# Bf16 parts that add up in PSUM, and a first spread whose chain of steps reaches over three groups, in a four-layer graph network on one core

## The reference

```
# 1: three message layers (l = 0, 1, 2)
m = relu(concat([x[src], x[dst], ew]) @ edge_W[l] + edge_b[l])
agg = segment_sum(m, dst)
x = relu(concat([x, agg]) @ node_W[l] + node_b[l])
# 2: eight relations
h0 = relu(x @ W_enc + b_enc)
agg = segment_sum(einsum('nd,rdo->rno', h0, W_rel)[etypes, src], dst)
out = h0 + relu(agg + h0 @ W_self + bias)
# 3: twice, a mean over the neighbours
agg = segment_sum(h[src], dst) * inv_deg[:, None]
h = relu(agg @ Wl + b + h @ Wr)
# 4: two layers of attention with two heads
h = layernorm(ent)
scores = leaky_relu(s_h[src] + s_t[dst] + s_r[edge_type])
A = 0.85 * segment_softmax(scores, src)
Z = h for both heads
for _ in range(3):
    Z = segment_sum(A[:, :, None] * Z[dst], src) + 0.15 * h
ent = Z.reshape(n, 128) @ W_o[l] + x
```

## Time and profile before

| What | Value |
|---|---|
| Time, median of 3 runs | 15644.12 us (15627.54 to 15644.18) |
| The profiled execution's own time | 15644.36 us |
| Its span, first to last instruction | 15642.6 us |
| PE busy | 13044.7 us, 83% |
| PEld busy | 11579.5 us, 74% |
| DVE busy | 11612.7 us, 74% |
| ACT busy | 4436.1 us, 28% |
| POOL busy | 2355.9 us, 15% |
| Mean granted TensorE clock | 0.907 |

### The profile page before, as it was taken

How to read it: one execution, slowest core, us unless ns; L and a number is a source line. 1 busy time by engine, 2 the same in 40 slices (tenths; PEclk the granted TensorE clock), 3 DMA queues, 4 the chain that set the end, 5 groups by cost and what they waited for, 6 DMA issues and landing times. The chain is left out here.

```text
span 15642.6 us, 488871 instructions
## 1 busy us (share of the span) xinstructions
PE 13044.7 (83%) x112911; PEld 11579.5 (74%) x112912; DVE 11612.7 (74%) x41655; ACT 4436.1 (28%) x16100; POOL 2355.9 (15%) x7659
## 2 busy tenths in 40 slices
PE   3444698998986999999867889899997788889998
PEld 2444587887875999989833778789993377778998
DVE  5444697997984888767679555589998955558999
ACT  1000122221221222222223232345542322224554
POOL 2777000000000000000000010112220000001221
PEclk9999998998996999999989786799998977779999
DMA  1111342442430111222235222222224522222222
GB/s 50 46 47 40 92 115 77 114 114 77 114 90 13 39 39 36 68 59 70 56 105 145 71 63 58 63 65 73 71 64 115 142 60 61 59 59 65 73 71 63
DMA packets 1260835, 1134.60 MB, mean 73 GB/s; under 512 B 224351, under 2 KB 1240800, under 8 KB 1260106
## 3 DMA queue, kind: packets, MB, share of 16 engines
q1 hardware_dynamic: 1234954, 1130.19, 27.5%
q0 software_dynamic: 25792, 3.35, 0.2%
HBM read 1115.06 MB, written 17.86 MB: 72 GB/s over the span
## 5 line engine op out<-in xcount | busy, mean ns | idle before, releaser
L965 DVE TENSOR_SCALAR hotT<-idx,iota_col 128x512 bf16<-128x512 f16 (+1 forms) x6000 | 1870.5, 365 | 605.9 <-PE G L1173 372.5
L1578 PE MATMUL G<-u_b,hotT 128*128 x6000 | 1682.2, 388 | 487.1 <-DVE msgs L1489 436.7
L972 DVE TENSOR_SCALAR hot<-iota_row,place 128x128 f32<-128x128 f16 (+1 forms) x9000 | 1909.8, 276 | 23.7 <-PE acc L1181 1.7
L1721 ACT ACTIVATE msgs<-G,share 128x64 f32<-128x64 f32 x6000 | 1394.6, 315 | 1346.6 <-PE G L1735 1346.1
L1578 PEld LDWEIGHTS G<-u_b,hotT 128*128 128x128 f32 x6000 | 1136.7, 237 | 671.0 <-issue 666.6
L1735 PE MATMUL G<-u_b,hotT 128*128 x12000 | 1591.1, 276 | 50.0 <-DVE hotT L1669 50.0
L1057 PE MATMUL G<-table_m,hotT 128*128 x9000 | 1424.2, 248 | 194.2 <-DVE sums L1079 166.5
L1745 PE MATMUL S<-msgs,hot 128*128 128x128 f32 x12000 | 1586.0, 275 | 0.0
L1735 PEld LDWEIGHTS G<-u_b,hotT 128*128 128x128 f32 x12000 | 1466.3, 193 | 50.7 <-issue 50.7
L1745 PEld LDWEIGHTS S<-msgs,hot 128*128 128x128 f32 x12000 | 1461.9, 192 | 0.0
L1069 PE MATMUL acc<-msgs,hot 128*128 128x102 f32 x9000 | 1386.5, 277 | 0.5 <-ACT msgs L1087 0.5
(11 more groups left out here) (321 smaller groups left out, 22667.8 us busy)
## 6 DMA issues: line engine op xcount, KB each, us to landing
idx<-pos_rows SPq DMA_DIRECT2D x7875, 128.0 KB
key_b<-key_rows SPq DMA_DIRECT2D x62, 416.0 KB
ty_b<-type_rows SPq DMA_DIRECT2D x62, 416.0 KB
rows<-rel_rows SPq DMA_DIRECT2D x1500, 6.0 KB
ew_now<-ew_rows_d SPq DMA_DIRECT2D x1125, 3.0 KB
sorted_d<-recs,place POOLq DMA_INDIRECT x806
sorted_d<-empty SPq DMA_DIRECT2D x4, 1500.0 KB
e<-sorted_d SPq DMA_DIRECT2D x1, 6000.0 KB
```

The lines of the kernel that those rows point to most:

```text
L965: op = eng.tensor_scalar(hotT[:, c % 2, n], idx[:, c, r], p.col[:, first:first + 1], None, ALU.is_equal)
L972: op = eng.tensor_scalar(hot[:, c % 2, q], p.row16[:], place[:, c % 2, q:q + 1], None, ALU.is_equal)
L1578: eng.matmul(G[c % 2][:, at_k:at_k + W], hotT[:, c % 2, q * P:(q + 1) * P], table[:, ds(dst_at(at, q, 24 * W), W)], start=True, stop=False)
L1721: op = eng.activation(msgs[:, c % 2, 2 + j // HEADS, j % HEADS * D:(j % HEADS + 1) * D], G[c % 2][1][:, j * D:(j + 1) * D], ACT.Copy, scal ...
```

## The change

1. **Message passes.** A gather is no longer three matmuls of 192 columns for a chunk but seven of 64: for each side the three parts are multiplied one after the other and add up in the same 64 columns of `G`. The edge weight keeps one matmul, of 64 columns: `ew_now` carries nine rows (three parts of the weight by three parts of its coefficient, `we9`), so the step's DMA brings nine rows. DVE's tensor reduce goes, and with it `sums` and the semaphore `taken`; ACT applies the relu to all four chunks in one instruction. A step is no longer cut in halves (H = 1).
2. **`relation_pass` becomes `parts_pass`**, with messages of 64 columns, not 102, and ACT writes them in one contiguous run for each chunk. The neighbour passes use it too: `sage_net` splits the table into three bf16 parts ahead of each pass, gathers in bf16 with 192 columns and scatters the three parts (12 bf16 matmuls in a step in place of four fp32 ones).
3. **First spread.** Four `G` tiles of one bank take turns in place of two of two banks; the gather of step t waits for the products of step t - 4. ACT does all products (eight instructions in a step), for step t - 2, and the exponential of step t - 1; DVE bends and subtracts for step t - 1; the scatter belongs to step t - 3. The own terms and the relation's are matmuls of 64 columns; the columns that are not needed are zero or not read.
4. **Later spreads.** The table is split into three bf16 parts ahead of each pass (`table_u`), `hotT` is bf16, and a gather is three bf16 matmuls of 128 columns for a chunk in place of one fp32 matmul.

```
-EW = 3
+EW = 9
...
             for q in range(4):
+                G = env["G"][c % 2][:, q * D:(q + 1) * D]
                 for side in range(2):
+                    of = dst_at(at, q, LAST) * 2 if side else src_at(at, 24 * 3 * D)
+                    for i in range(3):
+                        eng.matmul(G, env["hotT"][:, c % 2, side, q * P:(q + 1) * P], s.table3[side][:, ds(of + i * D, D)],
+                                   start=(side + i == 0), stop=False)
+                mm = eng.matmul(G, s.ew_now[:, c, q * P:(q + 1) * P], s.we9[:, l, :], start=False, stop=True)
...
         def scalar(eng, t, c, env):
+            env["later"](eng, env["gathered"], env["g0"], t + 1)
+            env["later"](eng, env["scattered"], env["sc0"], t - 3)
+            eng.activation(msgs[:, c, :, 0:D], env["G"][c % 2][:, 0:4 * D].rearrange("p (k f) -> p k f", f=D), ACT.Relu
+                           ).then_inc(env["made"].h, 1)
...
+def parts_pass(p, s, row, tables):
+        msgs = p.sb("msgs", [P, 4, 2, 3, D], BF16, ctx)
...
         for i in range(2):
-            neighbour_pass(p, s, s.cat[:].rearrange("p b f -> p (b f)"))
+            on_vector(p, [lambda e: e.tensor_copy(u[:], a)])
+            split_stage(p, u[:], [wide[:].rearrange("p (b q f) -> p b q f", q=3, f=D)[:, :, q, :] for q in range(3)])
+            parts_pass(p, s, s.pos_rows[0], [wide])
...
-        G = [p.ps("G", [P, 1024], ctx) for _ in range(2)]
+        G = [p.ps("G", [P, 512], ctx) for _ in range(4)]
...
                 def step(t, c):
+                    if not isinstance(t, int) or t > 1:
+                        product(t - 2, (c - 2) % 4)
                     if not isinstance(t, int) or t > 0:
-                        product(t - 1, (c - 1) % 4)
+                        share(t - 1, (c - 1) % 4)
                     pick(t, c)
-                    share(t, c)
...
+                    reach(eng, made, m0, t - 3)
+                    for q in range(4):
+                        to = G[c][:, q * W:(q + 1) * W]
+                        eng.matmul(to, hotT[:, c % 2, q * P:(q + 1) * P],
+                                   table[:, ds(dst_at(at, q, 24 * W), W)], start=True, stop=False)
+                        for i in range(3):
+                            eng.matmul(to[:, D:2 * D], near[:, c % 2, q * P:(q + 1) * P],
+                                       s.own[:, ds(src_at(at, 24 * SMALL) + i * 2 * HEADS, D)], start=False, stop=False)
+                        mm = eng.matmul(to[:, D:2 * D], rows[:, c, q], s.picks[:], start=False, stop=True)
...
-        hotT = p.sb("hotT", [P, 2, 4 * P], FP32, ctx)
+        hotT = p.sb("hotT", [P, 2, 4 * P], BF16, ctx)
+        table = p.sb("table_u", [P, BLK * 3 * W], BF16, ctx)
+        split_stage(p, out, [table[:].rearrange("p (b q f) -> p b q f", q=3, f=W)[:, :, q, :] for q in range(3)])
...
-                            mm = eng.matmul(G[c % 2][b][:, k * W:(k + 1) * W], hotT[:, c % 2, q * P:(q + 1) * P],
-                                            table[:, ds(dst_at(at, q, 24 * W), W)], start=True, stop=True)
+                            for i in range(3):
+                                mm = eng.matmul(G[c % 2][b][:, k * W:(k + 1) * W], hotT[:, c % 2, q * P:(q + 1) * P],
+                                                table[:, ds(dst_at(at, q, 24 * W) * 3 + i * W, W)], start=(i == 0), stop=(i == 2))
```

More of the change, by code:

```diff
@@ L1063, in gather @@
             return mm
         def scatter(eng, c, h, at, env):
-            j = (2 * (c - 1) + h) % 4
-            for k in range(2):
-                q = 2 * h + k
-                mm = eng.matmul(env["acc"][:, ds(dst_at(at, q, LAST), WIDE)], env["hot"][:, (c - 1) % 2, q, :], msgs[:, j, k, :],
-                                start=False, stop=False, skip_group_check=True)
-            return mm
-        def vector(eng, t, c, env):
-            for h in range(2):
-                j = (2 * c + h) % 4
-                env["later"](eng, env["made"], env["m0"], t * 2 + h - 3)
-                env["later"](eng, env["gathered"], env["g0"], t * 2 + h + 1)
-                eng.tensor_reduce(sums[:, j], env["G"][h][:, 0:6 * D].rearrange("p (k q f) -> p k f q", q=3, f=D),
-                                  AX.X, ALU.add).then_inc(env["taken"].h, 1)
@@ L1082, in scalar @@
-        def scalar(eng, t, c, env):
-            for h in range(2):
-                j = (2 * c + h) % 4
-                env["later"](eng, env["taken"], env["t0"], t * 2 + h + 1)
-                env["later"](eng, env["scattered"], env["sc0"], t * 2 + h - 3)
-                eng.activation(msgs[:, j, :, 0:D], sums[:, j], ACT.Relu).then_inc(env["made"].h, 1)
+            for q in range(4):
+                mm = eng.matmul(env["acc"][:, ds(dst_at(at, q, LAST), WIDE)], env["hot"][:, (c - 1) % 2, q, :],
+                                msgs[:, (c - 1) % 4, q, :], start=False, stop=False, skip_group_check=True)
@@ L1123, in scatter @@
                 for part in range(3):
-                    mm = eng.matmul(env["acc"][:, ds(dst_at(at, q, LAST), WIDE)], env["hot"][:, (c - 1) % 2, q, :],
-                                    msgs[:, j, k, part], start=False, stop=False,
-                                    skip_group_check=True)
+                    mm = eng.matmul(env["acc"][:, ds(dst_at(at, q, LAST), D)], env["hot"][:, (c - 1) % 2, q, :],
+                                    msgs[:, j, k, part], start=False, stop=False, skip_group_check=True)
             return mm
@@ L1133, in scalar @@
                 env["later"](eng, env["scattered"], env["sc0"], t * 2 + h - 3)
-                op = eng.copy(msgs[:, j, :, :, 0:D], env["G"][h][:, 0:6 * D].rearrange("p (k q f) -> p k q f", q=3, f=D))
+                op = eng.copy(msgs[:, j].rearrange("p k q f -> p k (q f)"),
+                              env["G"][h][:, 0:6 * D].rearrange("p (k f) -> p k f", f=3 * D))
                 op.then_inc(env["made"].h, 1)
-        edge_pass(p, s, [s.pos_rows[2]], None, 1, BF16, 0, FIVE, [(0, r) for r in range(RELS)], gather, scatter,
+        edge_pass(p, s, [row], None, 1, BF16, 0, FIVE, [(0, r) for r in range(NT)], gather, scatter,
                   lambda c: [p.ps("G", [P, 512], c) for _ in range(2)], None, scalar, {"scalar": sums_out(p, s)},
@@ L1419, in first_spread @@
             turned, hots, placed, shared, scattered, folded, termed, bends, lessed, kept))
-        g0, m0 = [x.at for x in gathered], [x.at for x in made]
+        g0, m0 = gathered.at, made.at
         on_vector(p, [lambda e: e.memset(rows[:], 0.0)])
@@ L1509, in _ @@
                 quarters(eng, step)
+                scatter_hots(Q - 2, (Q - 2) % 4)
+                bend(Q - 1, (Q - 1) % 4)
+                lessen(Q - 1, (Q - 1) % 4)
                 scatter_hots(Q - 1, (Q - 1) % 4)
-                product(Q - 1, (Q - 1) % 4)
-                for t in range(Q - 3, Q):
-                    fold(t, t % 4)
+                for t in range(Q - 4, Q):
+                    fold(t, t % 4, block_of(t))
                 turned.at += Q
@@ L1518, in _ @@
                 folded.at += Q + 1
-                made[0].at += Q
                 eng.wait_ge(folded.h, folded.at)
@@ L1566, in _ @@
                 shared.at += Q
-                made[1].at += Q
+                made.at += Q
             @block.tensor
@@ L1599, in step @@
                     gather(t, c, load_words(p, eng, 2, t, 1))
-                    if not isinstance(t, int) or t >= 2:
-                        scatter(t - 2, (c - 2) % 4)
+                    if not isinstance(t, int) or t >= 3:
+                        scatter(t - 3, (c - 3) % 4)
                 quarters(eng, step)
-                for t in range(Q - 2, Q):
+                for t in range(Q - 3, Q):
                     scatter(t, t % 4)
                 scattered.at += Q
-                for b in range(2):
-                    gathered[b].at += Q
+                gathered.at += Q
 def spread_pass(p, s, out):
     ctx = ExitStack()
-    table = out.rearrange("p b f -> p (b f)")
     W = HEADS * D
```

156 lines of the change are left out of this document (52 added, 104 removed).

## The result

The changed kernel takes **16,743.5 us** (median of 3 runs, 16,737.5 to 16,750.4) against 15,644.1: the ratio is 1.0707, interval 1.0682 to 1.0731. That is 1099 us slower; 1069 were forecast, and the time lies in the range. The profiled execution has a span of 16,748.7 us beside the 15,642.6 of before.

What follows compares the result with a forecast made beforehand. It took PE's sequencer (0.118 us an address) to bound the changed message passes and later spreads, and a ring of waits the old first spreads: 1200 + 1264 - 60 - 100 - 1245 + 10 = +1069, so 16,710 us, range 16,250 to 17,400.

Steps and rivals of the forecast that it cites:

- The price of an address: PE's sequencer: 0.118 us for each address instruction, read from four matmuls in the maximum pass.
- Message passes: Three passes: ten more address instructions a step, 3.40 us a step, +1200 us (bounds +1100 and +1340).
- Later spreads: Four passes: 12 addresses a step in place of 4, 2.60 us a step plus splits, +1264 us.
- Relation pass: Scatters of 64 columns, not 102, with PE being the bound: -60 us (0 to -75).
- Neighbour passes: Two passes: sequencer sets the step, 1.75 us against 1.91, less copy and splits: -100 us (+20 to -300).
- First spreads: Two passes: ring cut, PE sets the step at 2.75 us, full clock: -1245 us (-1340 to -910).
- the 5% added for waits that still meet: First spreads: allowance on PE's 2.62 us a step, giving 2.75.
- the ring: First spread: gather, pick, bend, exponential, product, gather of the step after next; cutting it lets PE set the step.
- The clock: Rival: thinly filled PE gets 1.2 GHz; +860 us in all spreads at all times, 17,570 us; chance in the spreads 0.07.
- The rival of hidden addresses: Whole kernel: sequencer runs ahead, engines decide; 13,130 us; chance 0.08 in full, 0.06 in part.
- The start: Ahead of the first message pass: nine rows of weights in place of three, twelve DMAs more, +10 us.
- The sum: Whole kernel: all parts together +1069 us on 15644.4, so 16,710 us, 6.8% more.

Runs made afterwards that it cites:

- narrow_own: Kernel of both_undone with the first spreads' score matmuls at their old widths (4 and 2 columns, not 64): 14,367.3 us, ratio 0.9046.
- ring_again: Changed kernel, but in the first spreads PE's gather of step t waits for products of step t - 2, not t - 4: 18,121.5 us.
- ring_narrow: Kernel of ring_again with the score matmuls also at their old widths, 4 and 2 columns: 18,082.4 us.
- msg_sums: Changed kernel with only the three message passes written as before (192-column gathers, reduce on DVE, three rows of weights): 15,503.3 us.
- both_undone: Changed kernel with its message passes and four later spreads written as before: 14,157.6 us, ratio 0.9058 to the kernel before.

## Why the prediction was right, step by step

**The price of an address** was right, and the sum rests on it. 0.118 us was read from four matmuls in another pass; the two runs with fewer addresses bear it out, with 0.122 between starts in the later spreads and 0.127 for each in the message passes. That the sequencer had nearly nothing to spare in the message passes was right too: ten addresses raised the step by 1.08 us where their price by the forecast is 1.18; that the rest is PE's wait for the sums, 0.16 a step, which is gone, was not tested by itself.

**Message passes**, +1200 forecast and +1227 measured: right. One reading in it was wrong. DVE's rest was worked out as its busy time less the reduce, 847.8 - 389.9. The groups of DVE overlap, however: 389.9 + 325.8 + 227.2 is 943 us beside a busy time of 848. What is left without the reduce is the other two groups, 559 us, as it came. It cost nothing, since DVE is far from the bound. ACT's work in the first spread was worked out in the same way, 2.24 us a step, and came as 2.01.

**Later spreads**, +1264 and +1331: the mechanism was right and the term too small. A step takes 2.64 us and not 2.60; the split has its place in the 14 us more ahead of the first matmul, as forecast. The term stood between its bounds.

**Relation pass**, -60 and -35. The price of a 64-column matmul was right: six of them take 0.34 us, (0.34 - 0.193) / 5 = 0.029. What was wrong was to take PE as the only bound. Timeline of PE in the relation pass after:

```profile
6224.91 1.48 PE L1101 MATMUL G<-wide,hotT 128*128 x16
6226.23 0.34 PE L1111 MATMUL acc<-msgs,hot 128*128 128x64 bf16 x6
6226.78 1.69 PE L1101 MATMUL G<-wide,hotT 128*128 x16 [0.21 <-issue]
...
6228.48 1.48 PE L1101 MATMUL G<-wide,hotT 128*128 x16
...
6229.97 1.48 PE L1101 MATMUL G<-wide,hotT 128*128 x16
```

Halves start 1.49 us apart where nothing comes between (6228.48 to 6229.97), and 1.87 where PE waits for issue (6224.91 to 6226.78), so part of the 0.2 us that PE was spared in a step went to its sequencer. Half was gained.

**Neighbour passes**, -100 and -64: a step takes 1.78 us, not 1.75, and the stretch of 715 us that the sum set it against holds 6 us around the pass. The two splits with the copy take 17 us as against 19. That it isn't PE's work is shown by the four steps above; which wait beside the addresses makes the 0.03 was not tested.

**First spreads**, -1245 and -1380: the mechanism was right, the size wrong mostly by the 5% added for waits that still meet. There are none: 2.62 us was PE's sum, 2.595 was measured. Here, where each handover has a whole step and PE never runs dry, the waits needed no allowance. The forecast gave the ring's cutting all the gain and full clock; the runs show that cutting it alone is enough for both, since narrow_own keeps 0.99, although 209 of the 1380 us hang on the clock alone in the ring.

**The clock** fell in the message and neighbour passes, to 0.89 and 0.78, as its rival had it, and cost little, as the prediction worked out: PE has time to spare there. In the spreads it stayed at 0.99 to 1.00. The prediction took it that idle time and the lower level go together in the ring; ring_again, idle for 423 of 1535 us at 0.99, shows that idle time alone doesn't bring it. The rival's price for all spreads at all times, +860, was too low as summed: it holds the four later spreads and the message passes, and leaves out the first spreads, whose 2.62 us a step would double too. The rival of hidden addresses was a little too high: 3 x 375 x 1.74 is 670 less for the message passes, not 640. The Trainium skill, same page, section "Part 1: The HAM clock gate", puts the throttle down to how busy PE has been. By the share of busy time alone the pair of rings isn't explained: at the full clock their steps have nearly the same length and the same number of matmuls, and one kept that clock while the other, with the narrower matmuls, did not.

**The start**: +27 and not +10. The nine rows make 15 to 17 us of it (the first message pass starts at 1759.6 in ring_narrow and at 1744.7 in msg_sums, on one chip, and 1999.0 in ring_again and 1982.1 in narrow_own on another). Another 12 come and go between executions: both_undone, with three rows, starts at 1755.9.

**The sum** came within 37 us of the measured one, and that closeness is in part luck: the message passes, the later spreads, the relation and neighbour passes and the start came out 172 us above their forecasts together, and the first spreads 135 below theirs. The range, 16,250 to 17,400, was wider than the size errors needed.

## What to carry to other kernels

Where a loop's operands are found at run time, count the addresses that PE's sequencer must work out as a resource of its own, beside the engine's time: splitting one fp32 matmul, or one wide one, into three bf16 parts with an address each triples them, and here it paid only where the parts shared an address. To find a ring, look for waits that follow each other in every step while no engine is busy throughout; letting the gather wait for products two steps older, with the buffers for it, was worth 1134 of the 1380 us here, where the passes in which only work was saved brought 103. Before a group is subtracted from an engine's busy time, add the groups up and see whether they overlap.

## What the runs showed of the hardware

- Matmuls that each need an address of their own started 0.118 us apart where PE was idle in between (maximum pass), 0.122 in the later spreads, and each address added 0.127 us to a message step. A 64-column bf16 matmul takes 0.029 us of PE and a 128-column one 0.055, so streams with an address for each are held at a quarter or a half of PE's rate.
- The granted clock was 0.99 and 1.00 in the ring with 64 columns and 423 us of idle in 1535, and 0.80 and 0.75 with 4 columns. In the neighbour pass it was 0.78 with 64 columns and 0.95 with 102, with no change of the time.
- One of the three chips needed some 235 us more ahead of the first message pass, and the same time as the others from there on. It arises in the loop that sorts the edges, between 229 and 1530 us in ring_narrow: the same loop is 234.5 us longer in ring_again, and the DMA engines moved 58.7 MB there at 39 GB/s, and 58.6 MB at 46 in ring_narrow. Why they did is open.
